# Attention's value products: one burst for each query tile instead of two

## What is computed

```
x1 = relu(layernorm(L_norm @ x @ Wc + bc)) + x
q, k, v = x1 @ Wq, x1 @ Wk, x1 @ Wv                    # split into H heads of hd
scores = einsum('bhnd,bhmd->bhnm', q, k) / sqrt(hd)
scores = where(adjacency > 0, scores, -1e9)
attn = softmax(scores, axis=-1)
o = einsum('bhnm,bhmd->bhnd', attn, v)                 # the value products
x2 = layernorm(x1 + o @ Wo + bo)
out = x + layernorm(x2 + gelu(x2 @ W1 + b1) @ W2 + b2)
```

## Time and profile before

| | before |
|---|---|
| median of 3 runs | 911.24 us |
| profiled execution | 910.41 us |
| its span | 908.5 us |
| TensorE busy | 862.2 us (95%) |
| VectorE busy | 652.3 us (72%) |
| ScalarE busy | 541.3 us (60%) |
| GpSimd busy | 327.1 us (36%) |

### The profile page before, as it was taken

The page is one execution under the profiler, slowest core; times in us unless marked ns, Lnnn a source line. Parts: engine busy times, 40 slices in busy tenths (PEclk is TensorE's granted clock), DMA queues, the critical chain, the costliest instruction groups (busy, mean ns, idle before and its releaser), DMA issues.

```text
span 908.5 us, 19047 instructions
## 1 busy us (share of the span) xinstructions
PE 862.2 (95%) x6765; PEld 705.9 (78%) x6765; DVE 652.3 (72%) x2110; ACT 541.3 (60%) x1234; POOL 327.1 (36%) x426
## 2 busy tenths in 40 slices
PE   6999999999999999987999999999999999999993
PEld 5779999998989888975777777767777777667883
DVE  6855564645453546535889888899898888987996
ACT  3134343434243233225888888888888888886884
POOL 4111111111111212301445545555455454424886
PEclk9799999999999999999999999999999999999997
DMA  3000000000000000402445555444445554420122
GB/s 102 0 12 13 12 12 13 12 13 13 13 12 13 12 24 1 124 16 76 121 102 122 140 140 141 125 109 110 101 117 141 140 140 127 109 46 2 48 70 70
DMA packets 46428, 61.73 MB, mean 68 GB/s; under 512 B 3567, under 2 KB 21246, under 8 KB 46334
## 3 DMA queue, kind: packets, MB, share of 16 engines
q1 hardware_dynamic: 46034, 60.38, 26.0%
q10 hardware_dynamic: 300, 0.13, 0.1%
HBM read 39.53 MB, written 20.97 MB: 67 GB/s over the span
## 4 chain that ended last, share of the span: by engine, by line
PE 44%; DVE 3%; ACT 2%; issue 2%; DMA 1%; POOL 0%; SPq 0%; DVEq 0%; ACTq 0%; POOLq 0%
PE bank L1769 13%; PE bank L1789 8%; PE bank L1756 6%; PE bank L1831 4%; PE bank L1509 3%; PE bank L1491 2%; PE bank L359 2%; PE bank L1838 1%; PE bank L268 1%; PE bank L368 1%; PE bank L363 1%; DVE prob L1938 1%; PE bank L1472 1%; ACT prob L1881 1%; DMA q_stack<-bounce_k 1%
## 5 line engine op out<-in xcount | busy, mean ns | idle before, releaser
L1881 ACT ACTIVATE prob<-prob,low 128x512 f32<-128x512 f32 x256 | 183.9, 720 | 22.3 <-DVE low L1938 22.1
L1938 DVE CUSTOM_DVE_ANT_0 prob<-bank,mask 128x512 f32<-128x512 f32 x256 | 171.8, 686 | 20.1 <-PE bank L1756 18.5
L1769 PE MATMUL bank<-ident,prob 128*128 128x128 f32 x1024 | 160.8, 280 | 0.0
L1769 PEld LDWEIGHTS bank<-ident,prob 128*128 128x128 f32 x1024 | 115.0, 141 | 40.9 <-issue 24.5
L1864 ACT ACTIVATE probT<-bank 128x512 f32<-128x512 f32 x176 | 104.8, 595 | 39.7 <-PE bank L1769 38.7
L1756 PE MATMUL bank<-k_stack,q_stack 128*128 128x512 f32 x256 | 122.8, 480 | 4.8 <-DVE low L1938 3.3
L820 PE MATMUL bank<-B_hi,halves 128*128 128x384 f32 x384 | 107.4, 342 | 1.6 <-DVE halves L1183 1.1
L791 PE MATMUL bank<-halves,P3T_hi 128*128 128x256 f32 x512 | 95.4, 288 | 3.4 <-DVE halves L1201 2.2
L610 POOL TENSOR_SCALAR var_eps<-mv 128x4 f32<-128x4 f32 x16 | 3.6, 226 | 243.8 <-DVE mv L1127 243.8
L791 PEld LDWEIGHTS bank<-halves,P3T_hi 128*128 128x128 f32 x512 | 81.7, 194 | 5.8 <-DVE halves L1201 2.5
L1789 PE MATMUL bank<-probT,v 128*32 128x128 f32 x2048 | 82.2, 279 | 0.2 <-DVE probT L1925 0.2
(11 more groups left out here) (265 smaller groups left out, 1960.5 us busy)
## 6 DMA issues: line engine op xcount, KB each, us to landing
k_stack<-bounce_q SPq DMA_DIRECT2D x64, 256.0 KB, 5.0
q_stack<-bounce_k SPq DMA_DIRECT2D x64, 256.0 KB, 7.4
bounce_q<-k_parts SPq DMA_DIRECT2D x16, 512.0 KB, 2.8
bounce_k<-q_parts SPq DMA_DIRECT2D x16, 512.0 KB, 3.1
x_in<-in_x_dram SPq DMA_DIRECT2D x16, 256.0 KB, 2.8
out_dram<-probT SPq DMA_DIRECT2D x16, 256.0 KB, 2.3
y<-in_adj_dram SPq DMA_DIRECT2D x4, 256.0 KB, 3.7
W1s<-in_L_gnn_W_dram SPq DMA_DIRECT2D x1, 128.0 KB, 2.2
```

The lines of the kernel that those rows point to most:

```text
L1769: last = pe.transpose(psum[2 + u % 2][:, mt * P:(mt + 1) * P], prob[u % RING][:, mt * P:(mt + 1) * P], ident[:, :])
L1881: act.activation(prob[u % RING][:, :], prob[u % RING][:, :], ACT.Exp, bias=low[:, u % TURNED:u % TURNED + 1], scale=-1.0, accum_out=row_su ...
L1938: dve.tensor_tensor_reduce(prob[u % RING][:, :], psum[u % 2][:, :], mask[:, u // HEADS, :], 1.0, 3e38, ALU.add, ALU.min, low[:, u % TURNED ...
```

## The change

Two numbers change. A query tile's sixteen value products (four key tiles, four heads) stand in one call, in units 9 and 13 and in units 1 and 5 of the next round.

```diff
@@ -1419,8 +1419,8 @@
 AT_RINV, AT_SPREAD, AT_SPREAD_OUT, AT_O, AT_PROJ, AT_Z2 = 0, 3, 4, 8, 11, 12
 AT_Z2_MOMENTS, AT_Z2_STD = 3, 5
 TURN_LAG = 3
-VALUES_LAG = 7
-VALUES_STEP = 2
+VALUES_LAG = 9
+VALUES_STEP = 4
 DVE_COPIES = (0, 7, 11, 13, 15)
```

## The result

The changed kernel took 901.14 us (median; 899.49 to 901.70), the kernel before 911.12 us beside it: ratio 0.9888, 95% interval 0.9871 to 0.9905, 1.1% faster. The forecast was 900.7 us.

The account below looks back on a forecast made before the run. TensorE bounds each round from key product to output projection, other engines the rest. Rounds 2 to 14 give 13 x 0.72 = 9.4 us, with edge rounds 10.5: 899.9 us, plus 0.83 for the median, 900.7; range 897.5 to 906.6.

Parts of the forecast that it names:

- Price of a burst: TensorE's value products: two key tiles cost 0.72 us, a merged four 1.16 instead of 1.44, saving 0.28 a pair.
- First stretch: Key product L359 to output projection L1838, TensorE leading: 0.72 us sooner, 0.44 to unit 8's scores plus 0.28 from units 7 and 9.
- Second stretch: L1838 to the next L359, set by other engines: TensorE's 0.56 us saved counts nothing; its x1 wait grows from 0.33 to some 0.9.
- Rounds 1, 15 and 16: Edge rounds: 0.28 us in round 1, 0.44 in round 15 (stack's DMA starts sooner), perhaps 0.4 in round 16.
- Sum: All rounds: 13 x 0.72 = 9.4 us for rounds 2 to 14, with the edge rounds 10.5 us together.
- The range: Whole kernel: 897.5 us (13 us saved) to 906.6 us, from the whole gain's side to VectorE's pace.
- The rule on the sequencer's pace: TensorE issues an instruction in no less than about 20 cycles: a double burst 1.07 us against 1.01, up to 4 us in all.
- VectorE's pace: Rival: VectorE's chain to unit 8's scores does not move, only 0.28 us a round counts; 906.6 us, chance 17%.
- TensorE's time counting whole: Rival: the part from L1838 to the next L359 shrinks too, 17.6 us saved; 893.6 us, chance 9%.
- The slower one: Rival: double bursts in units 13 and 1 starve or block, second half at half pace, about 0.5 us a round; 918 us, 7%.

Follow-up runs that it names:

- the run with the halved stack: Changed kernel with half of the last batch's stack left out of round 15's eight DMAs, against the kernel before: 899.11 us, ratio 0.9871.
- the run with tiles 1 and 2: Kernel before with only query tiles 1 and 2 merged (units 13 and 1), tiles 0 and 3 left in two bursts: 911.15 us, ratio 1.0002.
- the run with ScalarE's wait: Changed kernel with query tile 0's burst in unit 11, behind the output projection, and ScalarE's copy of unit 8 waiting for it: 910.23 us.
- the last run: Changed kernel with VectorE's z_std ahead of its copy of unit 11 and GpSimd's add of bo moved to its round's end: 907.71 us.

## Why the prediction was right

- *Price of a burst.* 0.72, 1.16 and 0.28 us: measured 1.16 in the changed kernel (and so 0.28 saved by each merged pair), 0.51 for one key tile. The row of 32 records in the trace before was the price of the new burst, and all but one of the merged pairs were charged at it.
- *First stretch, 0.72 us.* Measured 0.76, made of 0.47 for tile 3 (0.44 forecast, through ScalarE's copy, q_hi and L395) and 0.30 for tile 0 (0.28). Each was shown alone. As forecast, the scores of unit 8 show no wait any more.
- *Second stretch, nothing.* Measured 0.06 us a round, and done alone it makes no difference in time that can be told (ratio 1.0002). But what I said would be late next was wrong: TensorE's wait for x1 did not grow to 0.9 us, it fell to 0.21. The time went to the scores of unit 1, issued in unit 0 (0.37 us for the row minimum of VectorE at 617.57); the double burst of unit 1 then used up the rest. The text contradicted itself here: it had also said that scores cannot run more than a unit ahead, and that TensorE would be some 0.13 late behind the double burst, which leaves 0.33 - 0.13 = 0.20 of the wait. That sentence was right, the 0.9 was not.
- *Rounds 1, 15 and 16.* Round 1 gave 0.28 as forecast (25.15 to 24.87). Rounds 15 and 16 gave 0.08 instead of 0.84: the term for the edge rounds was wrong. I took round 15's 0.44 from the DMA's start; the last load of the stack landed at the same time in both kernels and held the scores at 18.07 and 18.08 us, and behind it stood VectorE and the double burst. Round 16 gave 0.09 for 0.4: TensorE's wait for VectorE grew by 0.47 us, and the double burst came behind it.
- *Sum.* 10.5 us forecast, 10.56 us measured over the rounds (10.48 + 0.08). That the two agree so closely is luck: rounds 2 to 14 gave 10.20 us, 0.78 each instead of 0.72, which is 0.8 us more than forecast, and the edge gave 0.8 us less.
- *The range.* Its lower end, 897.5 us, is called 13 us saved; from the median of 911.24 it is 13.7. Nothing hangs on it here.
- *The rule on the sequencer's pace* (the Trainium skill, Runtime: NRT & Kernel Launch, Instruction fetch mechanics) would, by the prediction's estimate, have cost each double burst up to 0.06 us. In this trace they take 1.01 us, like the row before, and in the run with the halved stack also right behind a released wait (786.91 to the next start at 787.92); the rule did not bind here.
- *Rivals.* VectorE's pace: its 0.28 us a round was tile 0's part alone; the chain did move. TensorE's time counting whole: refuted by the run with tiles 1 and 2. The slower one: no double burst ran at half pace. A double burst costs time where TensorE waits right ahead of it, and only rounds 15 and 16 are like that.

## What to carry to other kernels

Split a round at the points where one engine takes the lead from another, and count a saving only in the stretch where that engine leads: here half of the edit carried nine tenths of its gain. Where small products with another array form stand among full ones, the price is paid at each change of form (0.27 us there and back), so they want to stand together, provided that no engine waits behind the longer burst. Take what a wait costs from the starts around it, as with any other price: the idle time that the profile prints fell short of it (0.77 against 1.09 us a round). Before moving work out of the leading stretch, look at where in the other stretch the slack lies, and at what a burst was covering in its old place.

## What the runs showed of the hardware

- Two changes of the array's form cost 0.27 us together, with the granted clock at 1.00, the 2.4 GHz level: 0.09 ahead of the burst (0.41 instead of 0.32 us from the scores before it), the rest behind it.
- VectorE's L340, the same instruction on the same shape, took different times where GpSimd did other work beside it. The line in the changed kernel, in the run with ScalarE's wait, and in the last run (least, median and largest duration in ns):

```profile
L340 DVE SCALAR_TENSOR_TENSOR x<-z_norm,h x16: 683/1066/1071, 353.5 to 770.4; 128x512 f32<-128x512 f32 x16
```

```profile
L340 DVE SCALAR_TENSOR_TENSOR x<-z_norm,h x16: 680/793/1066, 355.4 to 781.7; 128x512 f32<-128x512 f32 x16
```

```profile
L340 DVE SCALAR_TENSOR_TENSOR x<-z_norm,h x16: 681/1455/1466, 352.5 to 776.7; 128x512 f32<-128x512 f32 x16
```

The 1.46 us are those beside add_bo (1.29 us on GpSimd), and GpSimd's copy of the inverse sums behind it took 1.08 us instead of 0.60. The Trainium skill (SBUF — State Buffer, Who interferes with whom) has VectorE operations with two SBUF inputs take turns with GpSimd at a shared port; the trace agrees in kind. No run here was made to separate it from other causes.
